# A Mamba-style decoder layer in which VectorE reads du from SBUF, Silu is one activation, and GpSimd's products have a new place

## The chip, the cores and the metric

The kernel runs on 1 core of one Trainium2 chip. The metric is the device time of one execution in microseconds (us). The kernel before was timed three times: 1171.12, 1177.21 and 1181.13 us, median 1177.21.

## The reference, cut to what matters

One decoder layer with four sequences (batches) of 512 tokens and 512 features: a selective state space block, then an attention over the context, then a linear layer with weights and rows quantized to integers; behind each an addition and a layer norm. The change touches the first block alone.

```python
proj = einsum('blh,he->bel', x, W_in)
hidden, gate = split(proj, 2, axis=1)              # E = 1024 channels each
hidden = silu(causal_conv4(hidden) + conv_bias)
dt, B, C = split(einsum('ble,ed->bld', hidden.T, W_x), [128, 144])
dts = softplus(dt @ W_dt + b_dt)                   # (b, l, E)
dA  = exp(dts[..., None] * A)                      # A: E x 16 states
dBu = dts[..., None] * B[:, :, None, :] * hidden[..., None]
state = dA * state + dBu                           # along the 512 tokens
y = einsum('ben,bn->be', state, C)
out = ((y + hidden * D) * silu(gate)) @ W_out
```

## The kernel before

The state scan has 4 x 1024 x 16 rows of 512 tokens. It is cut into 128 units, 32 a batch (UNITS). A unit is 32 channels of one batch with their 16 states: 128 partitions are 32 channels x 4 states, and the 4 (NJ) columns of 512 tokens hold the other states. Four units make the 128 channels of a block e (8 blocks a batch).

For one unit u:
- SyncE copies the 32 rows of dts and of du = dts * hidden from `steps` four times into `rep[u % REPS]` (`repeat`, line 348), by DMA.
- ScalarE computes dA in four exponentials (`exps`, line 581), one unit ahead of VectorE (AHEAD = 4 exponentials), and copies du from `rep` to the PSUM bank `du_rep` (`spread`, line 592). There is one such bank: the copy for u+1 waits until VectorE has finished the products of u.
- VectorE (`unit`, line 787) multiplies du, broadcast over two columns, by B from the SBUF tensor `Bb` into the PSUM tensor `dBu`, twice (line 798), and then runs two scans of 1024 elements (line 804) into `st[u % RING]`, with RING = 6.
- GpSimd multiplies each half of `st` by C from `Cb` in place (line 464).
- After four units TensorE sums the states in `state_sum` (line 927) with small matmuls into a bank `dense`.

All engines walk the same list of steps (b, g): step g of batch b goes with unit 32b + g + 1. What else a step does is in `items` (line 66), from tables of positions: projections "h" and "g" of the next and the current batch, the convolution "c" (four matmuls on TensorE from `pj`), "z" (softplus of the steps of a block on ScalarE, then du on GpSimd, line 492), the state sum "y", and for the batch before the output product "wo", attention ("q", "k", "en", "at", "xt", "av") and the quantized product ("qt", "ff"). Each such product takes one of BANKS = 3 PSUM banks in turn. In each step an engine does the unit's work first, then pending work of the last step, then the items.

Silu is built from tanh, since x * sigmoid(x) = x/2 * (1 + tanh(x/2)). For a gate ScalarE does tanh, the halving and the plus one (lines 698, 699, 701) and GpSimd the product (503). For a convolution ScalarE does the same three (565, 566, 568) and GpSimd the product one step later (478). For the first batch the convolution runs on VectorE (line 773) with taps and bias halved ahead of it (831, 832), then tanh and plus one (548, 550) and GpSimd's product. The exponentials, the softplus and the tanh need activation tables: a load stands in the program where the needed set is not the active one.

The first unit of batches 1 to 3 (STAGED = 1) takes B and C from the two halves of `wide`, since `Bb` and `Cb` can be loaded only once the last unit of the batch before is through (`load_bc`, line 340). As soon as VectorE and GpSimd have read `wide` for this unit (semaphores `s_mul` and `s_p`, line 394), SyncE loads w_out (2 MB) into it (`load_w_out`, line 337). TensorE needs it for "wo" at g = 2, and VectorE adds that product to the rows in `add_rows` (line 763). All the DMAs of this stretch stand in SyncE's one queue.

## Time and profile before

| what | value |
|---|---|
| median of 3 timed executions | 1177.21 us (1171.12 to 1181.13) |
| the profiled execution | 1177.67 us |
| its span, first to last instruction | 1175.9 us |
| mean granted TensorE clock | 0.859 of full speed |
| instructions in the profile | 10334 |
| packets of DMA, bytes | 66684, 135.03 MB |

The profile is of one execution. Busy shares are of the span. PE is TensorE, DVE is VectorE, ACT is ScalarE, POOL is GpSimd, SP is SyncE. A line number is that of the kernel before. In a group, the last columns are the idle time of the engine just ahead of these instructions and what ended most of it. A timeline row merges neighbours of one group: "4.45 ... x2" is the time from the start of the first to the end of the second.

### The profile page before, as it was taken

Reading aid. Unit: us, or ns where it says so; the run is one execution under the profiler, and the core shown is the slowest. Engines: PE = TensorE matmul, PEld = TensorE weight load, DVE = VectorE, ACT = ScalarE, POOL = GpSimd, SP = SyncE. Lnnn points to the kernel's source line nnn. Section 1 sums busy time; section 2 is a strip of 40 time slices with the busy share of each in tenths; the row PEclk is TensorE's granted clock in tenths of the full one; section 3 lists DMA queues with packets and bytes.
Section 4 is the critical chain, followed back from the end, with each engine's and each line's share of the span. In section 5 each row is a group of like instructions: output and inputs, shape, how many; then the busy total and the mean of one; then the engine's idle time right before and its main releaser. Section 6 shows DMA issues by size and latency. Waiting matters only on the chain.

```text
span 1175.9 us, 10334 instructions
## 1 busy us (share of the span) xinstructions
PE 856.8 (73%) x2708; PEld 335.0 (28%) x2718; DVE 973.5 (83%) x783; ACT 792.3 (67%) x1336; POOL 774.6 (66%) x483
## 2 busy tenths in 40 slices
PE   7923488878369789976639789878629856666994
PEld 2311133322023233432214234333203323222331
DVE  2469999898789987888979987898878999999733
ACT  3456677776456886886647777785666677777446
POOL 2228777777567766778656775777666777686533
PEclk9976698889679999998769898998868978777997
DMA  5184444453972334253893343344594353225100
GB/s 177 36 198 104 103 113 110 107 137 86 242 205 67 102 92 108 72 146 83 214 261 77 85 110 80 88 121 108 132 274 102 75 153 91 63 63 143 28 0 37
DMA packets 66684, 135.03 MB, mean 115 GB/s; under 512 B 13120, under 2 KB 19392, under 8 KB 66624
## 3 DMA queue, kind: packets, MB, share of 16 engines
q1 hardware_dynamic: 65904, 134.28, 45.0%
q8 instruction: 22, 0.36, 0.1%
q14 instruction: 38, 0.31, 0.1%
q10 hardware_dynamic: 720, 0.08, 0.0%
HBM read 62.75 MB, written 4.46 MB: 57 GB/s over the span
## 4 chain that ended last, share of the span: by engine, by line
PE 26%; issue 25%; DVE 20%; ACT 15%; DMA 7%; POOL 5%; SPq 1%; DVEq 0%; ACTq 0%; POOLq 0%
PE dense L906 16%; DVE st L804 14%; PE dense L962 6%; ACT dA L589 5%; POOL st L464 4%; DMA rep<-steps 3%; DMA wide<-w_out 3%; DVE dBu L798 2%; PE dense L939 2%; ACT squares L620 1%; DVE hs L782 1%; DVE x L763 1%; ACT L577 1%; ACT du_rep L597 1%; PE dBu L916 1%
## 5 line engine op out<-in xcount | busy, mean ns | idle before, releaser
L464 POOL TENSOR_TENSOR st<-st,Cb 128x1024 f32<-128x1024 f32 x250 | 584.3, 2359 | 216.5 <-DVE st L804 173.7
L804 DVE TENSOR_TENSOR_SCAN st<-dA,dBu 128x1024 f32<-128x1024 f32 x256 | 570.0, 2268 | 0.3 <-ACT dA L589 0.3
L589 ACT ACTIVATE dA<-rep,Aneg 128x511 f32<-128x511 f32 x512 | 328.0, 710 | 84.7 <-DMA rep<-steps 56.4
L798 DVE TENSOR_TENSOR dBu<-du_rep,Bb 128x1024 f32<-128x1024 f32 x250 | 294.4, 1223 | 78.9 <-ACT du_rep L597 46.4
L906 PE MATMUL dense<-xTs,Win 128*128 128x512 f32 x512 | 239.4, 612 | 14.2 <-DMA xTs<-xT 7.8
L939 PE MATMUL dense<-st,sel 128*32 128x512 f32 x1024 | 131.1, 657 | 52.1 <-POOL st L464 52.1
L906 PE MATMUL dense<-wide,hs 128*128 128x512 f32 x256 | 122.0, 633 | 61.9 <-DMA wide<-w_out 39.2
L906 PEld LDWEIGHTS dense<-xTs,Win 128*128 128x128 f32 x512 | 97.6, 195 | 147.3 <-issue 146.6
L962 PE MATMUL dense<-pj,Win 128*128 128x512 f32 (+1 forms) x192 | 105.5, 701 | 34.2 <-DVEq L785 20.7
L597 ACT COPY du_rep<-rep 128x512 f32<-128x512 f32 x128 | 74.3, 581 | 57.0 <-DVE dBu L798 48.6
L503 POOL TENSOR_TENSOR ta<-ta,tb 128x512 f32<-128x512 f32 x32 | 41.1, 1284 | 77.4 <-ACT tb L701 77.4
L906 PEld LDWEIGHTS dense<-wide,hs 128*128 128x128 f32 x256 | 51.0, 204 | 131.0 <-issue 68.1
L939 PEld LDWEIGHTS dense<-st,sel 128*32 128x32 f32 x1024 | 32.2, 119 | 149.6 <-issue 85.0
L962 PEld LDWEIGHTS dense<-pj,Win 128*128 128x128 f32 x192 | 42.2, 228 | 95.1 <-issue 95.0
L478 POOL TENSOR_TENSOR hs<-tb,ta 128x512 f32<-128x512 f32 x32 | 40.7, 1272 | 38.9 <-ACT tb L550 38.9
L933 PE MATMUL dense<-hs,Ddiag 128*128 128x512 f32 x64 | 38.0, 679 | 30.2 <-DVEq L785 22.4
L630 ACT ACTIVATE x<-x,nmean,rstd 128x512 f32<-128x512 f32 x36 | 28.8, 814 | 43.9 <-POOL nmean L472 43.9
L698 ACT ACTIVATE tb<-dense 128x512 f32<-128x512 f32 x32 | 19.0, 593 | 52.7 <-PE dense L906 48.0
L924 PE MATMUL dense<-ident,small 128*128 128x128 f32 x128 | 23.8, 318 | 41.4 <-ACT small L638 29.5
L492 POOL TENSOR_TENSOR steps<-steps,hs 128x512 f32<-128x512 f32 x32 | 40.7, 1271 | 19.6 <-ACT steps L577 19.6
L906 PE MATMUL dense<-wide 128*128 128x512 f32 x96 | 46.2, 626 | 6.2 <-ACTq L579 5.4
L906 PE MATMUL dense<-hs,wide 128*128 128x512 f32 x80 | 42.5, 687 | 11.1 <-issue 10.3
(112 smaller groups left out, 845.4 us busy)
## 6 DMA issues: line engine op xcount, KB each, us to landing
rep<-steps SPq DMA_DIRECT2D x512, 128.0 KB, 2.7
Win<-w_in SPq DMA_DIRECT2D x64, 256.0 KB, 2.7
wide<-w_out SPq DMA_DIRECT2D x4, 2048.0 KB, 16.4
Win<-w_conv SPq DMA_DIRECT2D x24, 256.0 KB, 2.6
wide<-bc_rows SPq DMA_DIRECT2D x24, 256.0 KB, 6.3
xTs<-xT SPq DMA_DIRECT2D x4, 1024.0 KB, 10.8
Bb<-bc_rows SPq DMA_DIRECT2D x16, 256.0 KB, 11.1
Cb<-bc_rows SPq DMA_DIRECT2D x16, 256.0 KB, 12.2
```

Of the source, the lines that this page charges most:

```text
L464: nc.gpsimd.tensor_tensor(s, s, C[:, j, :], ALU.mult).then_inc(s_p, 1)
L478: nc.gpsimd.tensor_tensor(hs[:, kb % 2, i, :], tb[:, m, :], ta[:, m, :], ALU.mult).then_inc(s_hs, 1)
L492: nc.gpsimd.tensor_tensor(steps[:, n % 3, 1, :], steps[:, n % 3, 0, :], hs[:, kb % 2, i, :], ALU.mult).then_inc(s_du, 1)
L503: nc.gpsimd.tensor_tensor(a, a, t, ALU.mult).then_inc(s_gate, 1)
L589: nc.scalar.activation(dA[:, u % 2, j, 1:T], rep[:, u % REPS, 0, 1:T], ACT.Exp, scale=Aneg[:, u % UNITS, j:j + 1]).then_inc(s_dA, 1)
L597: nc.scalar.copy(du_rep[:], rep[:, u % REPS, 1, :]).then_inc(s_duf, 1)
L798: V.tensor_tensor(dBu[:, j, :], du_rep[:].unsqueeze(1).to_broadcast([P, JH, T]), B[:, j, :], ALU.mult).then_inc(s_mul, 1)
L804: V.tensor_tensor_scan(st[:, u % RING, j, :].rearrange("p j t -> p (j t)"), dA[:, u % 2, j, :].rearrange("p j t -> p (j t)"), dBu[:, j, :] ...
L906: mm = nc.tensor.matmul(ps[0:rows, :], lhsT, rhs, start=n == 0, stop=n == len(pairs) - 1)
L933: nc.tensor.matmul(ps, Ddiag[:, e, :], hs[:, b % 2, e, :], start=True, stop=False)
L939: mm = nc.tensor.matmul(ps[32 * q:32 * q + 32, :], sel[:, 0:32], st[:, (4 * n + q) % RING, j, :], start=False, stop=j == NJ - 1)
L962: mm = nc.tensor.matmul(ps[:, k:T], Win[:, n % 3, k, :], pj[:, 0:T - k], start=k == 0, stop=k == KC - 1)
```

## The change

- VectorE's products read du from `rep` in SBUF; `spread`, `du_rep` and its semaphore are gone. `rep` has 4 buffers instead of 3, and the buffer is free when VectorE's products are done.
- The PSUM bank of `du_rep` becomes a fourth bank `dense`.
- Silu is one activation for the convolutions (in both forms) and for the gate; the halvings, the plus ones, the tensor `tb` and GpSimd's products `hs` and `ta` are gone.
- GpSimd's product for the first half of a unit keeps its place. The one for the second half stands at the end of the step, behind norms, du and the bias, and waits until VectorE has finished both products of the next unit.

```diff
-BANKS = 3
-REPS = 3
+BANKS = 4
+REPS = 4
...
-                    sp.wait_ge(s_duf, u - REPS + 1)
+                    sp.wait_ge(s_mul, NH * (u - REPS + 1))
...
+            def weigh_states(u, h):
+
+                C = spread_at(pool, u, s_cc, 1, Cb)
+                pool.wait_ge(s_scan, NH * u + h + 1)
+                if h and u + 1 < NB * UNITS:
+                    pool.wait_ge(s_mul, NH * (u + 2))
+                j = slice(JH * h, JH * h + JH)
+                s = st[:, u % RING, j, :]
+                nc.gpsimd.tensor_tensor(s, s, C[:, j, :], ALU.mult).then_inc(s_p, 1)
...
-                    C = spread_at(pool, u, s_cc, 1, Cb)
-                    for h in range(NH):
-                        pool.wait_ge(s_scan, NH * u + h + 1)
-                        j = slice(JH * h, JH * h + JH)
-                        s = st[:, u % RING, j, :]
-                        nc.gpsimd.tensor_tensor(s, s, C[:, j, :], ALU.mult).then_inc(s_p, 1)
+                scanned = 0 <= u < NB * UNITS
+                if scanned:
+                    weigh_states(u, 0)
...
-                for kb, i in pending:
-
-                    pool.wait_ge(s_tanh, 2 * (NE * kb + i + 1))
-                    m = temp[("c" if kb else "h", kb, i)] % TEMPS
-                    nc.gpsimd.tensor_tensor(hs[:, kb % 2, i, :], tb[:, m, :], ta[:, m, :],
-                                            ALU.mult).then_inc(s_hs, 1)
...
-                        pool.wait_ge(s_gt, 3 * (n + 1))
-                        nc.gpsimd.tensor_tensor(a, a, t, ALU.mult).then_inc(s_gate, 1)
-                        pool.wait_ge(s_gate, n + 1)
                     if key in norm:
                         rows.append(key)
+                if scanned:
+                    weigh_states(u, 1)
...
-                nc.scalar.activation(t, ps, ACT.Tanh, scale=0.5, bias=cb[:, i:i + 1]).then_inc(s_tanh, 1)
-                nc.scalar.activation(a, ps, ACT.Identity, scale=0.5, bias=cb[:, i:i + 1]).then_inc(free, 1)
-                act.wait_ge(s_tanh, n + 1)
-                nc.scalar.activation(t, t, ACT.Identity, bias=ones[:, 0:1]).then_inc(s_tanh, 1)
+                nc.scalar.activation(hs[:, b % 2, i, :], ps, ACT.Silu, bias=cb[:, i:i + 1]).then_inc(s_hs, 1)
+                act.wait_ge(s_hs, NE * b + i + 1)
+                act.sem_inc(free, 1)
...
-            def spread(u):
-
-                act.wait_ge(s_rep[u % REPS], 64 * (u // REPS + 1))
-                if u:
-                    act.wait_ge(s_mul, NH * u)
-                nc.scalar.copy(du_rep[:], rep[:, u % REPS, 1, :]).then_inc(s_duf, 1)
...
-                        nc.scalar.activation(t, ps, ACT.Tanh, scale=0.5).then_inc(s_gt, 1)
-                        nc.scalar.activation(a, ps, ACT.Identity, scale=0.5).then_inc(s_gt, 1)
-                        act.wait_ge(s_gt, 3 * n + 2)
-                        nc.scalar.activation(t, t, ACT.Identity, bias=ones[:, 0:1]).then_inc(s_gt, 1)
+                        nc.scalar.activation(temp_slot(key), ps, ACT.Silu).then_inc(s_gate, 1)
+                        act.wait_ge(s_gate, NE * kb + i + 1)
                         act.sem_inc(free, 1)
...
             def unit(u):
-                dve.wait_ge(s_duf, u + 1)
+                dve.wait_ge(s_rep[u % REPS], 64 * (u // REPS + 1))
...
-                    V.tensor_tensor(dBu[:, j, :], du_rep[:].unsqueeze(1).to_broadcast([P, JH, T]), B[:, j, :],
+                    V.tensor_tensor(dBu[:, j, :], rep[:, u % REPS, 1:2, :].to_broadcast([P, JH, T]), B[:, j, :],
                                     ALU.mult).then_inc(s_mul, 1)
```

The order on GpSimd at steps 10 to 12 of batch 0, the kernel before: du of a block (L492), the products with C (L464), and the products that finish a convolution (L478) and a gate (L503).

```order
L492 TENSOR_TENSOR steps<-steps,hs 128x512 [waits steps_ready]
L464 TENSOR_TENSOR st<-st,Cb 128x1024 [waits scan_done] x2
L478 TENSOR_TENSOR hs<-tb,ta 128x512 [waits tanh_done]
L503 TENSOR_TENSOR ta<-ta,tb 128x512 [waits hs_ready,gate_part]
L464 TENSOR_TENSOR st<-st,Cb 128x1024 [waits scan_done,gate_ready]
L464 TENSOR_TENSOR st<-st,Cb 128x1024 [waits scan_done]
L478 TENSOR_TENSOR hs<-tb,ta 128x512 [waits tanh_done]
```

The same place of the changed kernel, where L480 is du and L456 the products with C.

```order
L456 TENSOR_TENSOR st<-st,Cb 128x1024 [waits scan_done]
L480 TENSOR_TENSOR steps<-steps,hs 128x512 [waits hs_ready,steps_ready]
L456 TENSOR_TENSOR st<-st,Cb 128x1024 [waits dBu_done,scan_done]
L456 TENSOR_TENSOR st<-st,Cb 128x1024 [waits scan_done]
L456 TENSOR_TENSOR st<-st,Cb 128x1024 [waits dBu_done,scan_done]
```

du has moved between the two products of its unit, the second product of every unit waits for VectorE's products as well (dBu_done), and the products of the convolution and the gate are gone.

The order on ScalarE at steps 10 and 11 of batch 0, the kernel before: softplus (L577), convolution (L565 to L568), `pj` (L558), exponentials (L589), the copy of du (L597).

```order
L577 ACT_TABLE_LOAD
L577 ACTIVATE steps<-dense0,bdt 128x512
L565 ACT_TABLE_LOAD
L565 ACTIVATE tb<-dense1,cb 128x512
L566 ACTIVATE ta<-dense1,cb 128x512
L568 ACTIVATE tb<-tb,ones 128x512
L558 COPY pj<-dense2 128x512
L589 ACTIVATE dA<-rep,Aneg 128x511 x4
L597 COPY du_rep<-rep 128x512
```

The same place of the changed kernel (softplus L556, convolution L545, `pj` L540, exponentials L568, gate L663).

```order
L556 ACT_TABLE_LOAD
L556 ACTIVATE steps<-dense0,bdt 128x512
L545 ACT_TABLE_LOAD
L545 ACTIVATE hs<-dense1,cb 128x512
L540 COPY pj<-dense2 128x512
L568 ACT_TABLE_LOAD
L568 ACTIVATE dA<-rep,Aneg 128x511 x4
L545 ACT_TABLE_LOAD
L545 ACTIVATE hs<-dense3,cb 128x512
L663 ACTIVATE ta<-dense0 128x512
```

Two activations and the copy have gone, and a table load has come behind the convolution and ahead of the next one. Over the whole program the order has 63 loads before and 139 in the changed kernel.

The order on GpSimd at the first batch boundary of the changed kernel, where the first unit of the batch takes C from `wide`.

```order
L456 TENSOR_TENSOR st<-st,wide 128x1024 [waits scan_done,bc_staged]
L456 TENSOR_TENSOR st<-st,wide 128x1024 [waits dBu_done,scan_done,bc_staged]
L456 TENSOR_TENSOR st<-st,Cb 128x1024 [waits scan_done,c_spread]
```

The second product with `wide`, for which the load of w_out waits, now stands behind VectorE's products of the next unit, which need `Bb`.

## Rows read from the trace of the kernel before

**Rows 1.** The page, part 1; then one stretch: us, busy us by engine, PEclk, DMA, GB/s
```profile
PE 856.8 (73%) x2708; PEld 335.0 (28%) x2718; DVE 973.5 (83%) x783; ACT 792.3 (67%) x1336; POOL 774.6 (66%) x483
...
72.42:1119.20 1046.78, 761.46 (x2439) 297.20 (x2449) 930.20 (x698) 730.79 (x1216) 740.26 (x424) 0.85 0.48 120
```

**Rows 2.** Groups of instructions by line: busy us, mean ns, idle before
```profile
L804 DVE TENSOR_TENSOR_SCAN st<-dA,dBu 128x1024 f32<-128x1024 f32 x256 | 570.0, 2268 | 0.3 <-ACT dA L589 0.3
L798 DVE TENSOR_TENSOR dBu<-du_rep,Bb 128x1024 f32<-128x1024 f32 x250 | 294.4, 1223 | 78.9 <-ACT du_rep L597 46.4 <-DMA Bb<-bc_rows 17.1 <-DVE x L763 6.0
...
L464 POOL TENSOR_TENSOR st<-st,Cb 128x1024 f32<-128x1024 f32 x250 | 584.3, 2359 | 216.5 <-DVE st L804 173.7 <-DMA Cb<-bc_rows 40.9 <-POOL hs L478 0.4
...
L597 ACT COPY du_rep<-rep 128x512 f32<-128x512 f32 x128 | 74.3, 581 | 57.0 <-DVE dBu L798 48.6 <-DMA rep<-steps 8.4
```

**Rows 3.** Timeline 290 to 300 us, VectorE and GpSimd: start, us, what
```profile
290.32 2.34 DVE L798 TENSOR_TENSOR dBu<-du_rep,Bb 128x1024 f32<-128x1024 f32 x2
292.56 4.46 DVE L804 TENSOR_TENSOR_SCAN st<-dA,dBu 128x1024 f32<-128x1024 f32 x2
...
294.92 4.65 POOL L464 TENSOR_TENSOR st<-st,Cb 128x1024 f32<-128x1024 f32 x2 [1.86 <-DVE st L804]
```

**Rows 4.** Waits of VectorE, 72.42 to 1119.2 us: total, times, longest
```profile
DVE dBu L798 <- ACT du_rep L597: 49.4, 28, 10.8
DVE x L763 <- PE dense L906: 22.3, 5, 6.7
DVE dBu L798 <- DMA Bb<-bc_rows: 17.1, 3, 6.4
DVE dense L890 <- PE dense L906: 7.3, 4, 3.5
DVE x L763 <- issue: 6.6, 2, 3.3
```

**Rows 5.** Timeline 54 to 61 us, VectorE and GpSimd
```profile
54.67 1.01 DVE L756 TENSOR_SCALAR small<-x,winv 128x512 f32<-128x512 f32 x2
...
58.61 0.70 DVE L756 TENSOR_SCALAR small<-x,winv 128x512 f32<-128x512 f32 x1 [2.93 <-PE dense L924]
...
59.34 1.46 DVE L756 TENSOR_SCALAR small<-x,winv 128x512 f32<-128x512 f32 x1
...
57.75 1.27 POOL L492 TENSOR_TENSOR steps<-steps,hs 128x512 f32<-128x512 f32 x1 [4.01 <-ACT steps L577]
59.25 1.26 POOL L492 TENSOR_TENSOR steps<-steps,hs 128x512 f32<-128x512 f32 x1 [0.23 <-ACT steps L577]
```

**Rows 6.** GpSimd: groups by line, and a timeline row
```profile
L492 POOL TENSOR_TENSOR steps<-steps,hs 128x512 f32<-128x512 f32 x32 | 40.7, 1271 | 19.6 <-ACT steps L577 19.6
...
L470 POOL TENSOR_TENSOR rstd<-var,neghalf 128x1 f32<-128x1 f32 x48 | 26.5, 552 | 35.3 <-ACT var L623 35.3
...
L472 POOL TENSOR_TENSOR nmean<-nmean,rstd 128x1 f32<-128x1 f32 x48 | 9.2, 192 | 3.8
...
52.47 1.26 POOL L478 TENSOR_TENSOR hs<-tb,ta 128x512 f32<-128x512 f32 x1 [4.20 <-ACT tb L550]
```

**Rows 7.** Timeline at the first batch boundary, all engines
```profile
309.51 4.68 POOL L464 TENSOR_TENSOR st<-st,wide 128x1024 f32<-128x1024 f32 x2 [1.13 <-DVE st L804]
...
314.26 0.40 SPq L338 DMA_DIRECT2D wide<-w_out  x1
...
317.98 2.36 DVE L798 TENSOR_TENSOR dBu<-du_rep,Bb 128x1024 f32<-128x1024 f32 x2 [6.44 <-DMA Bb<-bc_rows]
...
341.85 0.69 DVE L763 SCALAR_TENSOR_TENSOR x<-dense,x 128x512 f32<-128x512 f32 x1 [2.98 <-PE dense L906]
```

**Rows 8.** ScalarE: timeline at a table load; the gate's plus one
```profile
471.74 1.28 ACT L577 ACT_TABLE_LOAD   x1
473.03 0.69 ACT L577 ACTIVATE steps<-dense,bdt 128x512 f32<-128x512 f32 x1
...
L701 ACT ACTIVATE tb<-tb,ones 128x512 f32<-128x512 f32 x32 | 23.1, 722 | 1.0
```

More of the change, by code:

```diff
@@ L50 @@
 HID_AT = [9, 10, 13, 14, 17, 18, 21, 22]
+CONV_AT = [10, 11, 14, 15, 18, 19, 22, 23]
 DT_AT = 25
@@ L84, in items @@
         keys.append(("z", (n + 2) // NE, (n + 2) % NE))
-    if after and b >= 0 and g - 1 in HID_AT:
-        keys.append(("c", b + 1, HID_AT.index(g - 1)))
-    if after and g in HID_AT:
-        keys.append(("h", b + 1, HID_AT.index(g)))
+    if after and b >= 0:
+        keys.extend(("c", b + 1, i) for i, at in enumerate(CONV_AT) if at == g)
+    if after:
+        keys.extend(("h", b + 1, i) for i, at in enumerate(HID_AT) if at == g)
     if b >= 1:
@@ L122, in decoder_layer @@
     turn = {key: (n % BANKS, n // BANKS) for n, key in enumerate(order)}
-    temp_keys = [key for key in order if key[0] in "gc" or key[0] == "h" and key[1] == 0]
+    temp_keys = [key for key in order if key[0] == "g" or key[0] == "h" and key[1] == 0]
     temp = {key: m for m, key in enumerate(temp_keys)}
@@ L485, in _ @@
                     n = NE * kb + i
-                    a, t = (x[:, temp[key] % TEMPS, :] for x in (ta, tb)) if key in temp else (None, None)
-                    if kind == ("c" if kb else "h"):
-                        pending = [(kb, i)]
-                    elif kind == "z":
+                    if kind == "z":
                         pool.wait_ge(s_dt, n + 1)
+                        pool.wait_ge(s_hs, n + 1)
                         nc.gpsimd.tensor_tensor(steps[:, n % 3, 1, :], steps[:, n % 3, 0, :], hs[:, kb % 2, i, :],
@@ L531, in temp_slot @@
                     else:
-                        act.wait_ge(s_temp, sum(k[0] != "g" for k in temp_keys[:m - TEMPS + 1]))
-                return ta[:, m % TEMPS, :], tb[:, m % TEMPS, :]
+                        act.wait_ge(s_hs, i + 1)
+                return ta[:, m % TEMPS, :]
             def hid_front(b, i):
                 ps, _ = full(("h", b, i))
-                a, _ = temp_slot(("h", b, i))
-                if b == 0 and i == 0:
-                    act.wait_ge(s_prep, 1)
+                a = temp_slot(("h", b, i))
+                if i == 0:
+                    act.wait_ge(s_conv_c, 32)
                 nc.scalar.activation(a, ps, ACT.Identity, scale=ck[:, i, KC - 1:KC],
@@ L546, in hid_back @@
                 act.wait_ge(s_conv, NE * b + i + 1)
-                t = tb[:, m, :]
-                nc.scalar.activation(t, ta[:, m, :], ACT.Tanh).then_inc(s_tanh, 1)
-                act.wait_ge(s_tanh, 2 * (NE * b + i) + 1)
-                nc.scalar.activation(t, t, ACT.Identity, bias=ones[:, 0:1]).then_inc(s_tanh, 1)
+                nc.scalar.activation(hs[:, b % 2, i, :], ta[:, m, :], ACT.Silu).then_inc(s_hs, 1)
             def projected(b, i):
@@ L657, in _ @@
                     first = NJ * (UNITS * b + g + 1)
-                    u = first // NJ
-                    if u == 0:
-                        spread(0)
                     for m in range(first + AHEAD if first else 0, min(first + NJ + AHEAD, NB * UNITS * NJ)):
                         exps(m // NJ, m % NJ)
-                    if u + 1 < NB * UNITS:
-                        spread(u + 1)
                 for args in pending:
```

21 lines of the change are left out of this document (1 added, 20 removed).

## The prediction

> **What bounds the kernel now.** I read the page's busy times first. VectorE is busy for 83% of the span, every other engine for 73% or less [rows 1]. The stretch that matters runs from the first product of a unit to the last scan, 72.4 to 1119.2 us: 1046.8 us, with VectorE busy for 930.2 of them [rows 1]. A unit is two products (state inputs dBu) and two scans [rows 2]. In the timeline the next product starts as the last scan ends: 290.32 to the scan at 292.56, and 4.46 us of scans [rows 3]; a unit costs about 6.64 us (2.26 to the scan, 4.38 to the next product), and 128 units 850 us. The other VectorE work in the stretch is 930.2 - 850 = 80 us. The remaining 117 us are waits. Their list [rows 4] shows the copy of du into PSUM first: 49.4 us in 28 places, of which the longest, 10.8, lies ahead of the stretch; so 38.6 inside. Then 22.3 + 7.3 + 6.6 = 36.2 us for products of TensorE, and 17.1 for Bb at the batch boundaries. So VectorE is the bound, and the copy the largest wait.
>
> **VectorE's source of du.** The copy goes: 128 on ScalarE (74.3 us, [rows 2]), which is no bound, and with it the waits of 38.6 us. They go whole: without the first they are 27 of 1.4 us on average, and come about because a copy is the last thing in ScalarE's step, behind the exponentials of the same unit. Now VectorE's product needs no engine but the DMA of `rep`, and only its scan, 2.3 us behind, needs the exponentials. The product itself keeps 1024 elements a lane. No product of that shape from two SBUF tensors is in the trace; between the 512-element operation of 486 ns [rows 5] doubled (0.97) and GpSimd's 2.36 us for the same shape [rows 2], I take its own 1.22 [rows 2], nearest by far.
>
> **The two engines' products.** What the change adds is that this product reads rep and Bb, both in SBUF, while GpSimd multiplies two SBUF tensors. One place shows what VectorE can suffer from that [rows 5]. A SBUF-to-SBUF operation of 512 elements takes 0.49 us at 54.67, GpSimd idle (two in 1.01). At 58.61 it takes 0.70 and ends 0.29 after GpSimd's product ends (57.75 + 1.27 = 59.02). The next starts at 59.34, takes 1.46 and ends at 60.80: again 0.29 after GpSimd's (59.25 + 1.26 = 60.51). So this kind waits for the end of a GpSimd operation, and 0.49 - 0.29 = 0.20 us of its own lead lie inside the wait. It has one tensor input, so it does not prove the case; from below the cost of such waits is nothing, and from above the full serial sum (below). I take it that they exclude each other, as the only rows on the question do.
> The Trainium skill, SBUF — State Buffer, "Who interferes with whom", speaks against the change: a VectorE instruction with two SBUF inputs contends with a GpSimd one that reads SBUF, and whichever comes second blocks until the first is over. By that rule the sum below stands; without it the first rival does. The trace agrees for the one-input kind (+0.29 us both times).
>
> The new order places GpSimd's second product of unit u behind both VectorE products of u+1, and small GpSimd work ahead of it. I follow a plain unit from the start S of its first scan. The last product ends at S + 0.10 (2.34 for the two against 2.24 to the scan, [rows 3]); GpSimd follows 0.1 later (it starts at 294.92 where the first scan ended at 292.56 + 2.27 = 294.83, [rows 2, 3]). Its pair takes 4.68 [rows 7], so GpSimd is done at S + 4.88, where VectorE was done at S + 4.45: it blocks 0.4 us. First product 1.22 - 0.20 later, S + 5.90; second 1.12 later, S + 7.02; next scan S + 6.93. Instead of 6.64, 6.93 us: 128 units take 887.
> Extras come on top. VectorE's (80 us) hide the 0.45 us that GpSimd lasts longer, wherever one stands: 53 us stay over, counted unit by unit along the order. GpSimd's lie between its two products of a unit, where VectorE wants the same exclusion: 30 products du of 1.27 (38 us), 12 additions of the bias of the same shape (15), 36 pairs of 0.55 and 0.19 for the norms (27) [rows 6]. They mostly fall on units where VectorE has no extra. All serial, where the larger of the two counts in a unit: 53 + 78 = 131; if the second and later one of a place slips beside the next scan, about half of the 42 us that are not du goes: 111. I take 111.
>
> **Waits that stay or come.** Bb 17. TensorE's 36: a fourth bank lets it run ahead, I take 10 off (between none and the 26 not at w_out), 26. At each of three boundaries the load of w_out waits for GpSimd's second product of the staged unit. Before, that ran from 309.51, and the load was issued at 314.26, ahead of VectorE's next product at 317.98, which waited for Bb. Now the product stands behind it: 317.98 + 2.36 + 2.36, so w_out is issued at 322.7, 8.4 us later. VectorE waited 2.98 us for the product with w_out at 341.85 [rows 7]; with fewer transfers beside it I take w_out 6 us later, half of it hidden by VectorE's own delay: 3 x 3 = 9. The load of Cb waits likewise, one product (2.4 us) later, which shifts GpSimd against a VectorE product: 3 x 2 = 6. At the start GpSimd begins late, behind the load of Cb (it waits 40.9 us in all for Cb, [rows 2]), and must catch up two units, each product against one of VectorE's: 4. Sum 62.
> Stretch: 887 + 111 + 62 = 1060 against 1046.8: +13.
>
> **ScalarE and Silu.** Each gate, and each convolution from the second batch on, falls from three activations to one (gate: tanh, half, plus one). The order has 139 table loads instead of 63. A load takes 1.28 us and the next activation starts 0.01 later [rows 8]: 76 x 1.283 = 98 us more. Against that stand the 74 of the copies [rows 2], and two activations less for each of the 32 gates and 24 convolutions: the plus one, 0.72 [rows 8], and the halving, at least the 0.58 of a copy of that shape [rows 2], 56 x 1.30 = 73. ScalarE gets no busier (98 against 147), and it is idle for 30% of the stretch (730.8 of 1046.8 busy, [rows 1]). Cost 0; the cover is that idle time and the lead of one unit that the exponentials have. If it is gone, a load (1.28) stands ahead of the exponentials and the scan waits for them.
> The Trainium skill, ScalarE: Activation LUTs, "What ACT_TABLE_LOAD costs", states some 1.38 us of drain beside each load; by it ScalarE would carry 105 us more. The row at 473.03 stands directly behind the load [rows 8], so this trace shows no drain there.
> In the head the last hs needs no plus-one (0.72) and no product on GpSimd (1.27) [rows 6, 8]: -2 us.
>
> **Sum.** Profiled execution 1177.7 (span 1175.9) + 13 - 2 = 1189, say 1190; the median of the three is 1177.2, half a microsecond lower, so nothing is moved for it.
>
> **Rivals.**
> - *No exclusion for two SBUF inputs.* For it: those rows show only the one-input kind. Then the copy's waits go and nothing replaces them: 1177.7 - 38.6 - 10 - 2, plus w_out late in full, 3 x 6 = 18: 1145. Chance 0.13.
> - *The exclusion is dearer.* GpSimd wins at every change of hands: all 131 us serial (+20), 0.1 us at each of 256 VectorE products (+26), TensorE's 10 not won: 1246; with half of it 1220. Against it: a waiting VectorE got in at once at 59.02 [rows 5]. Chance 0.25.
> - *The extras hide.* All of GpSimd's but du slip beside scans (-21): 1169. Chance 0.14.
> - *ScalarE becomes late* by its loads: a third of 98 us on the path, 1222. VectorE's waits before [rows 4] name no exponential. Chance 0.03.
> The forecast holds 0.45.
>
> **Numbers.** A measurement tells about 1% from no change, 12 us. Faster (below 1165): the first rival and a part of the third, 0.20. Same: 0.28, from the third and the lower part of the forecast's (1165 to 1189). Slower: 0.52. The range goes from the first rival, 1145, to 1228, between the two sizes of the second.
>
> **What would show it.** The products of VectorE (1.22 us) have a longer mean, about 1.5, with the first of each unit near 1.4 to 1.7 and ending 1.0 us after a GpSimd product; no wait for du is left; 139 loads of 1.28; w_out issued one VectorE and one GpSimd product behind Bb. If the products stay at 1.22 beside GpSimd, the first rival holds and the forecast is wrong. If waits for dA at scans appear, it is ScalarE.

## The result and the profile after

The changed kernel took 1164.9 us (median of four executions, 1162.72 to 1165.72) against 1178.8 us before in the same comparison (four, 1171.12 to 1181.13): a ratio of 0.990, interval 0.986 to 0.994. It is faster by 1%, where 1190 us and a loss of 1% were forecast. Its profiled execution took 1165.72 us.

The first part of its page, and below it the row for the stretch from the first product of a unit to the last scan, as in [rows 1]:

```profile
PE 830.5 (71%) x2708; PEld 327.9 (28%) x2718; DVE 1026.1 (88%) x781; ACT 759.5 (65%) x1164; POOL 748.2 (64%) x419
...
71.27:1107.80 1036.53, 736.50 (x2443) 290.64 (x2453) 983.23 (x698) 702.82 (x1053) 724.74 (x369) 0.87 0.48 121
```

The stretch fell from 1046.8 to 1036.5 us. VectorE's busy time in it rose by 53.0 us (930.2 to 983.2) with the same 698 instructions, and its idle time fell by 63.3 (116.6 to 53.3). That is nearly the whole result: 53 us of something that the records count as work, against 63 us of waits. ScalarE's busy time in the stretch fell, from 730.8 to 702.8.

The groups by line show where the 53 us lie. They answer to [rows 2, 6].

```profile
L767 DVE TENSOR_TENSOR_SCAN st<-dA,dBu 128x1024 f32<-128x1024 f32 x256 | 570.0, 2266 | 0.0
...
L761 DVE TENSOR_TENSOR dBu<-rep,Bb 128x1024 f32<-128x1024 f32 x250 | 344.9, 1423 | 37.9 <-DMA rep<-steps 10.9
...
L480 POOL TENSOR_TENSOR steps<-steps,hs 128x512 f32<-128x512 f32 x32 | 57.6, 1799 | 72.8 <-ACT steps L556 72.7
...
L469 POOL TENSOR_TENSOR rstd<-var,neghalf 128x1 f32<-128x1 f32 x48 | 49.4, 1028 | 42.5 <-ACT var L595 42.5
```

The scans are unchanged to 2 ns. The 250 products of VectorE went from a mean of 1223 to 1423 ns, which is 50 us. On the other side GpSimd's du went from 1271 to 1799 and its small rstd from 552 to 1028. A mean that rises for the same shape on two engines at once suggests that each stands still inside its own instruction. The timeline shows it: first VectorE, then GpSimd, 94 to 106 us.

```profile
94.94 2.72 DVE L761 TENSOR_TENSOR dBu<-rep,Bb 128x1024 f32<-128x1024 f32 x2
...
101.95 3.80 DVE L761 TENSOR_TENSOR dBu<-rep,Bb 128x1024 f32<-128x1024 f32 x2
...
90.80 4.64 POOL L456 TENSOR_TENSOR st<-st,Cb 128x1024 f32<-128x1024 f32 x2 [1.23 <-DVE dBu L761]
97.81 4.64 POOL L456 TENSOR_TENSOR st<-st,Cb 128x1024 f32<-128x1024 f32 x2 [2.37 <-DVE dBu L761]
102.41 2.25 POOL L480 TENSOR_TENSOR steps<-steps,hs 128x512 f32<-128x512 f32 x1
```

GpSimd's pair ends at 95.44, half a microsecond into VectorE's pair at 94.94; that pair takes 2.72 instead of 2.34 [rows 3]. The next GpSimd pair ends at 102.45, and du is queued right behind it. VectorE's pair at 101.95 gets its first product in, du waits meanwhile (2.25 instead of 1.27) and runs between the two products, and VectorE's pair takes 3.80. In these rows each engine waits for the end of the other's current instruction, then goes first. From here on this is called the block. Counted over the timeline, 58 of the 128 pairs took 2.3 to 2.4 us, 44 took 2.7 to 2.8 (0.4 more), four 3.0 to 3.2, 21 took 3.4 to 4.0, and one 6.10. All pairs together took 356 us, against 301 both in the kernel before and in the kernel that has the new place but whose products still read PSUM (place_alone, below).

All 21 long pairs come from a du. In 16 of them du lies inside the pair. In the other five du ran first and made GpSimd's two products with C late, so that the end of the second one falls into VectorE's pair. One of the five:

```profile
416.33 3.65 DVE L761 TENSOR_TENSOR dBu<-rep,Bb 128x1024 f32<-128x1024 f32 x2
...
411.87 1.27 POOL L480 TENSOR_TENSOR steps<-steps,hs 128x512 f32<-128x512 f32 x1 [2.63 <-ACT steps L556]
413.10 4.66 POOL L456 TENSOR_TENSOR st<-st,Cb 128x1024 f32<-128x1024 f32 x2
```

VectorE's waits in that stretch, which answer to [rows 4]:

```profile
DVE x L726 <- PE dense L866: 13.7, 5, 4.0
DVE dBu L761 <- DMA rep<-steps: 10.9, 1, 10.9
...
DVE x L726 <- issue: 6.3, 2, 3.5
DVE dBu L761 <- DMA Bb<-bc_rows: 6.1, 3, 3.7
DVE dBu L761 <- PE dense L899: 5.2, 3, 3.8
```

The wait for the copy is gone. The 10.9 for `rep` is one wait ahead of the first product and no part of the 53.3. Bb fell from 17.1 to 6.1. TensorE's two at `x` (13.7 + 6.3 = 20.0) stood at 28.9, and the 7.3 at L890 fell to 0.4 (now L850). The 5.2 for the state sums (L899) is the 5.3 that the kernel before has at L939 and that [rows 4] does not show.

A small part of the wait for du has come back in another form.

```profile
DVE dBu L761 <- issue: 5.1, 3, 2.2
```

The view names no cause for these three. The two longest end at 427.24 and 693.17 us, and the last DMA that fills `rep` for that unit lands at 426.89 and 692.76. So VectorE waits there for `rep` itself.

### The profile page after: what moved, and what is told of

It reads as the page before. It is cut to its first block, busy times and chain, and to the rows that moved or that the text cites. A ratio compares the mean times of both kernels' runs of the same rounds, so it can differ in the third digit from the quotient of the medians.

```text
span 1163.9 us, 10065 instructions
## 1 busy us (share of the span) xinstructions
PE 830.5 (71%) x2708; PEld 327.9 (28%) x2718; DVE 1026.1 (88%) x781; ACT 759.5 (65%) x1164; POOL 748.2 (64%) x419
## 4 chain that ended last, share of the span: by engine, by line
issue 35%; DVE 28%; PE 22%; DMA 6%; ACT 5%; POOL 2%; SPq 2%; DVEq 0%; POOLq 0%; ACTq 0%
DVE st L767 19%; PE dense L866 15%; DVE dBu L761 4%; PE dense L922 3%; DMA wide<-w_out 2%; DMA Bb<-bc_rows 2%; PE dense L899 2%; DVE x L726 1%; DVE hs L745 1%; POOL st L456 1%; PE dBu L876 1%; SPq L340 1%; DVE xsc L818 1%; DVE dense L850 1%; ACT squares L592 1%
## 5 line engine op out<-in xcount | busy, mean ns | idle before, releaser
L456 POOL TENSOR_TENSOR st<-st,Cb 128x1024 f32<-128x1024 f32 x250 | 584.5, 2360 | 279.3 <-DVE dBu L761 256.0
L568 ACT ACTIVATE dA<-rep,Aneg 128x511 f32<-128x511 f32 x512 | 329.3, 710 | 119.9 <-DVE st L767 110.7
L761 DVE TENSOR_TENSOR dBu<-rep,Bb 128x1024 f32<-128x1024 f32 x250 | 344.9, 1423 | 37.9 <-DMA rep<-steps 10.9
L899 PE MATMUL dense<-st,sel 128*32 128x512 f32 x1024 | 134.2, 665 | 112.8 <-POOL st L456 112.8
L922 PE MATMUL dense<-pj,Win 128*128 128x512 f32 (+1 forms) x192 | 94.5, 638 | 32.4 <-issue 22.2
L480 POOL TENSOR_TENSOR steps<-steps,hs 128x512 f32<-128x512 f32 x32 | 57.6, 1799 | 72.8 <-ACT steps L556 72.7
L899 PEld LDWEIGHTS dense<-st,sel 128*32 128x32 f32 x1024 | 31.0, 117 | 209.3 <-POOL st L456 134.7
L469 POOL TENSOR_TENSOR rstd<-var,neghalf 128x1 f32<-128x1 f32 x48 | 49.4, 1028 | 42.5 <-ACT var L595 42.5
L922 PEld LDWEIGHTS dense<-pj,Win 128*128 128x128 f32 x192 | 37.9, 205 | 86.8 <-issue 86.8
L884 PEld LDWEIGHTS dense<-ident,small 128*128 128x128 f32 x128 | 17.0, 162 | 105.4 <-ACT small L610 66.2
L726 DVE SCALAR_TENSOR_TENSOR x<-dense,x 128x512 f32<-128x512 f32 x36 | 24.7, 686 | 21.0 <-PE dense L866 13.7
L663 ACT ACTIVATE ta<-dense 128x512 f32<-128x512 f32 x32 | 19.1, 597 | 33.2 <-PE dense L866 32.7
```

The costliest lines, as they stand in the source:

```text
L456: nc.gpsimd.tensor_tensor(s, s, C[:, j, :], ALU.mult).then_inc(s_p, 1)
L469: nc.gpsimd.tensor_tensor(rstd[:, c], var[:, c], neghalf[:], ALU.pow).then_inc(s_rstd, 1)
L480: nc.gpsimd.tensor_tensor(steps[:, n % 3, 1, :], steps[:, n % 3, 0, :], hs[:, kb % 2, i, :], ALU.mult).then_inc(s_du, 1)
L568: nc.scalar.activation(dA[:, u % 2, j, 1:T], rep[:, u % REPS, 0, 1:T], ACT.Exp, scale=Aneg[:, u % UNITS, j:j + 1]).then_inc(s_dA, 1)
L726: V.scalar_tensor_tensor(x_i, ps, 1.0, x_i, ALU.mult, ALU.add, accum_out=rowsum[:, n % 4:n % 4 + 1]).then_inc(s_sum, 1)
L761: V.tensor_tensor(dBu[:, j, :], rep[:, u % REPS, 1:2, :].to_broadcast([P, JH, T]), B[:, j, :], ALU.mult).then_inc(s_mul, 1)
```

## The experiments

The times are medians, the ratio is to the kernel before on the same chip, with its 95% interval. Two runs, marked so, are single executions. Sums of pairs, idle times and stretches are read from the one profiled execution of each kernel.

### Is the block real, and is it the source in SBUF?

**place_undone**: the changed kernel, but GpSimd's second product right behind the first, without its new wait.

```diff
             def weigh_states(u, h):
-                if h and u + 1 < NB * UNITS:
-                    pool.wait_ge(s_mul, NH * (u + 2))
...
                     weigh_states(u, 0)
+                    weigh_states(u, 1)
...
-                if scanned:
-                    weigh_states(u, 1)
```

> The changed kernel with GpSimd's second product of each unit put back directly behind the first, without the wait for VectorE's products. Theory A (exclusion, and the waiting VectorE gets in between two GpSimd products): VectorE's two products are split by one GpSimd product of 2.34 us, pairs near 4.9 instead of 2.75, some 2.2 us more for each of 128 units: 1165 + 200 to 280, about 1400. Rival B (VectorE keeps its turn for both products, or the place is of little worth): under 1200.

1306.3 us (one execution), 141 us above the changed kernel: 1.10 us a unit. VectorE, then GpSimd, from its timeline:

```profile
108.96 4.70 DVE L758 TENSOR_TENSOR dBu<-rep,Bb 128x1024 f32<-128x1024 f32 x2
...
106.94 5.63 POOL L454 TENSOR_TENSOR st<-st,Cb 128x1024 f32<-128x1024 f32 x2 [1.14 <-DVE st L764]
```

The pair takes twice its 2.34 us, and GpSimd's pair 5.63 instead of 4.65. GpSimd starts at 106.94 and ends its first product at about 109.3; VectorE, ready at 108.96, gets in then; GpSimd's second product, queued since 109.3, gets in between VectorE's two. Nothing in either instruction has changed against the changed kernel, only when they meet. Theory A had the mechanism right and the size too large: 61 of the 128 pairs took 4.6 to 5.0 us, where it expected all of them near 4.9. The pairs sum to 519 us, 162 more than in the changed kernel, and VectorE's waits fell by 18.

**place_alone**: the kernel before, du still copied to PSUM, with only the new place and wait of GpSimd's second product.

```diff
+                scanned = 0 <= u < NB * UNITS
+                if scanned:
+                    weigh_states(u, 0)
...
+                if scanned:
+                    weigh_states(u, 1)
```

> The kernel before (du copied to PSUM, tanh, three banks) with only the place of GpSimd's second product changed: behind the small work of the step and behind VectorE's products of the next unit. Theory A (exclusion needs two SBUF inputs; here VectorE's product has one): VectorE's products stay at 1.22 us, pairs at 2.34, though GpSimd's work of 1.27 us now lies beside them; the time moves only through later state sums and w_out, 1174 to 1190. Rival B (GpSimd's work stretches VectorE's products whatever their source): pairs of 2.7 us and more, and a time over 1200.

1176.3 us against 1177.95, 0.998 (0.997 to 1.000): the place alone is worth nothing. Its groups and its waits:

```profile
L805 DVE TENSOR_TENSOR dBu<-du_rep,Bb 128x1024 f32<-128x1024 f32 x250 | 294.3, 1223 | 74.0 <-ACT du_rep L604 40.7 <-DMA Bb<-bc_rows 17.2 <-DVE x L770 6.7
```
```profile
DVE dBu L805 <- ACT du_rep L604: 43.0, 22, 10.3
```

All 128 pairs took 2.3 or 2.4 us, the sum 301.4, as theory A expected, though GpSimd's products stand where they stand in the changed kernel. The cleanest comparison is with tanh_kept (below), which differs from this kernel only in the source of du (and with it the copy on ScalarE) and in the fourth bank: there the pairs sum to 415 us and the time is 1232.5. With du from PSUM there is no block; with both inputs from SBUF there is.

**narrow_products**: the changed kernel with GpSimd's products with C cut to one element a column. It leaves out nearly all of the products with C.

```diff
-                nc.gpsimd.tensor_tensor(s, s, C[:, j, :], ALU.mult).then_inc(s_p, 1)
+                nc.gpsimd.tensor_tensor(s[:, :, 0:1], s[:, :, 0:1], C[:, j, 0:1], ALU.mult).then_inc(s_p, 1)
```

> The changed kernel, but GpSimd's products with C take one column of each 512 instead of all (it leaves out nearly all of the products with C). Theory A (exclusion: VectorE's products are long, 356 us in all instead of 301, only because of GpSimd's operations): pairs of 2.37 nearly everywhere but beside du, the sum of VectorE's products falls to 310 to 320, the time to about 1125. Rival B (the product from two SBUF tensors is itself slower, or something else stretches it): pairs keep their 2.75 us. If the products shorten and the time stays over 1150, TensorE is the next bound.

1135.4 us (one execution), 29.5 below the changed kernel.

```profile
L456 POOL TENSOR_TENSOR st<-st,Cb 128x2 f32<-128x2 f32 x250 | 49.2, 198 | 777.3 <-DVE dBu L761 530.8 <-DVE st L767 209.5 <-DMA Cb<-bc_rows 29.0
...
L761 DVE TENSOR_TENSOR dBu<-rep,Bb 128x1024 f32<-128x1024 f32 x250 | 313.3, 1298 | 45.9 <-PE dense L899 12.9 <-DMA Bb<-bc_rows 12.5 <-DMA rep<-steps 9.9
```

The pairs now sum to 320 us, 36 less, and 114 of 128 are free of any block. In the stretch the time fell by 27 of these 36: nine came back as waits, mostly for TensorE (12.9 instead of 5.2) and Bb (12.5 instead of 6.1). So GpSimd's products with C cost the changed kernel about 27 us through the block; the rest of the 29.5 lies ahead of the stretch and behind it. The 19 us that remain above 301 lie in the 14 pairs of 3.2 to 4.2 us, all with a du, six of them with the bias as well. Theory A's sum (310 to 320) is met and rival B falls, since the same two products from SBUF take 2.3 to 2.4 us when GpSimd is out of the way; the time is 10 us above the 1125 expected.

### What Silu is worth

**silu_alone**: the kernel before, with Silu as one activation, in the changed kernel's steps for the convolutions, and nothing else (copy of du, three banks, three buffers).

```diff
-                nc.scalar.activation(t, ps, ACT.Tanh, scale=0.5, bias=cb[:, i:i + 1]).then_inc(s_tanh, 1)
...
+                nc.scalar.activation(hs[:, b % 2, i, :], ps, ACT.Silu, bias=cb[:, i:i + 1]).then_inc(s_hs, 1)
```

> The kernel before with Silu as one activation and the table of positions for the convolution, nothing else (the copy of du into PSUM, three banks and three rep buffers stay, GpSimd's second product stays directly behind the first). Theory A (the gain of the change lies in the copy of du and in VectorE's other waits; Silu is hidden apart from the head): 2 us less in the head and within 6 us of before otherwise, about 1176; VectorE's waits for the copy stay between 35 and 55 us. Rival B (the gain comes from ScalarE and GpSimd being freed of the tanh form): 1165 or less, the waits for the copy fall under 20 us.

1173.7 us against 1177.1, 0.995 (0.992 to 0.997). Theory A holds: a gain of 3.4 us where it expected about 2, and a wait for the copy that did not fall but grew, from 49.4 to 54.6. In the profiled executions the whole gain lies ahead of the stretch, which starts at 69.50 us instead of 72.42; the stretch itself is 1046.8 us long in both. Such a start is uncertain by itself: it lies at 71.27 in the changed kernel and at 68.79 in staged_now (below), whose program is the same up to there.

```profile
DVE dBu L772 <- ACT du_rep L575: 54.6, 34, 8.8
```

**tanh_kept**: the other half: du from `rep`, four banks (three buffers), the new place, but Silu still from tanh, with GpSimd's 64 products of 1.27 us for it.

```diff
-            def spread(u):
...
-                dve.wait_ge(s_duf, u + 1)
+                dve.wait_ge(s_rep[u % REPS], 64 * (u // REPS + 1))
...
+                if scanned:
+                    weigh_states(u, 1)
```

> The kernel before with the source of du, four banks and the new place of GpSimd's second product, but Silu as tanh as before and three rep buffers (a fourth does not fit beside tb). GpSimd keeps 56 products of 1.27 us for convolutions and gates. Theory A (each of them stands in VectorE's way like a product du, 0.8 to 1.1 us each, and Silu's worth in this change lies in that): 1205 to 1230. Rival B (Silu is worth what it is worth alone on the kernel before, 3 to 5 us): 1166 to 1172.

1232.5 us against 1175.7, 1.047 (1.044 to 1.050).

```profile
L791 DVE TENSOR_TENSOR dBu<-rep,Bb 128x1024 f32<-128x1024 f32 x250 | 403.8, 1659 | 40.0 <-DMA rep<-steps 9.9 <-DMA Bb<-bc_rows 8.3 <-DVE x L756 7.4
```
```profile
486.99 5.08 DVE L791 TENSOR_TENSOR dBu<-rep,Bb 128x1024 f32<-128x1024 f32 x2 [0.71 <-PE dense L932]
...
483.95 1.29 POOL L506 TENSOR_TENSOR ta<-ta,tb 128x512 f32<-128x512 f32 x1 [7.87 <-ACT tb L694]
485.31 5.66 POOL L459 TENSOR_TENSOR st<-st,Cb 128x1024 f32<-128x1024 f32 x2
```

The product with `ta` at 483.95 makes GpSimd's pair late; VectorE's pair at 486.99 falls on it and takes 5.08. The mean of VectorE's product is 1659 ns, 236 above the changed kernel's, 59 us over 250. Against the same kernel with Silu (reps3, below, 1163.2) it is 69 us slower, a little more than theory A's upper end. (GpSimd keeps 64 such products, 32 for convolutions and 32 for gates; the expectation counted 56.) So Silu is worth 3.4 us by itself and 69 beside the products from SBUF, and without it the change would have lost 5%. Nearly all of it acts through GpSimd, by taking 64 of its instructions away: against reps3 the pairs hold 60 us more and VectorE's waits 6, and no scan waits for dA.

### The wait for the copy

**copy_first**: the kernel before, with the copy of du ahead of the exponentials of its step instead of behind them.

```diff
+                        if m == max(first + AHEAD, NJ):
+                            spread(u + 1)
...
-                    if u + 1 < NB * UNITS:
-                        spread(u + 1)
```

> The kernel before with one thing moved: in ScalarE's step the copy of du for unit u+1 stands ahead of the four exponentials of u+1 instead of behind them. Theory A (most of the gain of the change is the wait for this copy, which came last in the step): the 38.6 us of waits inside the stretch fall to under 12, the time to about 1150, with VectorE's products at 1.22 us throughout. Rival B (these waits are those of a late ScalarE, so the scan's wait for the exponentials takes their place): within 1% of before, 1170 to 1182, with a new wait of scans for dA of 20 us or more.

1193.4 us, 1.011 (1.008 to 1.014). Both theories missed. First VectorE's waits, then ScalarE's group of the copy:

```profile
DVE dBu L798 <- PE dense L939: 33.2, 12, 3.8
...
DVE dBu L798 <- DMA Bb<-bc_rows: 22.9, 3, 8.2
...
DVE dBu L798 <- ACT du_rep L597: 12.4, 4, 8.8
```
```profile
L597 ACT COPY du_rep<-rep 128x512 f32<-128x512 f32 x128 | 75.1, 587 | 194.4 <-DVE dBu L798 160.2 <-DMA rep<-steps 33.5 <-ACT steps L577 0.7
```

The wait for the copy fell to 12.4 us, 8.8 of it ahead of the stretch, as theory A had it, but the time did not follow. The copy now holds ScalarE, 194 us in all (57.0 before, [rows 2]), mostly until VectorE has read the bank, and what stands behind it on ScalarE starts later. Rival B's new wait for dA is not there either (0.35 us at a scan). The waits of VectorE for TensorE's state sums appeared, 33.2 us. A cheaper cure of the wait in the old kernel than the changed source was thus not found here; where TensorE was held up was not traced further.

**silu_copy_first**: both together, 1175.9 us, 0.997 (0.995 to 1.000). The diff is that of the two above.

> Both of the two before: Silu as one activation, and the copy of du ahead of the exponentials. Theory A: the two add up, about 1148, faster than the changed kernel (1165), since nothing of VectorE's is blocked by GpSimd. Rival B: at best the changed kernel's time, 1165.

The copy's wait is 10.7 (one, ahead of the stretch), the state sums 27.5. With ScalarE relieved the same edit costs 2 us (against silu_alone) instead of 16, but still wins nothing; theory A, that the two add up to 1148, missed by 28 us.

### Banks, buffers, and the late w_out

**banks3** and **reps3**: the changed kernel with BANKS = 3, and with REPS = 3.

```diff
-BANKS = 4
+BANKS = 3
```

> The changed kernel with three dense banks instead of four (the fourth is left unused). Theory A (as predicted, the fourth bank is worth some 10 us): about 1175. Theory B (formed on the run with the copy ahead of the exponentials: with three banks TensorE comes late as soon as VectorE stops waiting for the copy, so the fourth bank carries most of the gain): 1185 or more, with VectorE waiting over 40 us more than in the changed kernel for TensorE (state sum L899 and the products).

> The changed kernel with three rep buffers instead of four. Theory A (a buffer is now held until VectorE's products are done, 2.3 us longer than for the copy; three are enough, since the DMA is issued two units ahead): within 3 us of the changed kernel, 1162 to 1168. Rival B: waits for rep at the batch boundaries, 5 us or more at each: 1180.

banks3 took 1172.7 us (0.996, 0.994 to 0.998), reps3 1163.2 (0.988, 0.985 to 0.991). The difference of the two is 9.6 us; against the changed kernel's own 1164.9, banks3 is 7.8 us slower. This is the worth of the fourth bank, since the fourth buffer of `rep` is worth nothing measurable. The first expectation of each run holds. In banks3:

```profile
DVE x L726 <- PE dense L866: 17.3, 5, 5.7
...
DVE dBu L761 <- PE dense L899: 15.4, 9, 3.8
```

against 13.7 and 5.2: the bank's worth is a wait for TensorE's state sums and one for its dense products.

**staged_now**: the changed kernel, where GpSimd's second product of a staged unit doesn't wait for VectorE's next products, so that w_out is loaded earlier.

```diff
-                if h and u + 1 < NB * UNITS:
+                if h and u + 1 < NB * UNITS and not (u and u % UNITS < STAGED):
```

> The changed kernel, but for the first unit of batches 1 to 3 (which reads the halves of wide) GpSimd's second product does not wait for VectorE's products of the next unit, so that the load of w_out is issued some 8 us earlier at three places. Theory A (the late w_out costs 3 us at each boundary, as in the prediction): 1156, and up to 18 us less (1147) if nothing hides it. Rival B (the load lands faster, w_out is not late for VectorE by more than before): within 3 us of the changed kernel, 1162 to 1168.

1164.5 us, 0.987 (0.984 to 0.991): the same as the changed kernel, as rival B expected. w_out is issued at 320.02 and there at 335.6, 15.6 us later. In the changed kernel, at the same boundary (to be set beside [rows 7]):

```profile
322.28 2.37 DVE L761 TENSOR_TENSOR dBu<-rep,Bb 128x1024 f32<-128x1024 f32 x2 [3.69 <-DMA Bb<-bc_rows]
324.82 2.34 POOL L456 TENSOR_TENSOR st<-st,wide 128x1024 f32<-128x1024 f32 x1 [5.78 <-DVE dBu L761]
...
327.23 0.40 SPq L333 DMA_DIRECT2D wide<-w_out  x1
...
336.93 9.27 PE L866 MATMUL dense<-wide,hs 128*128 128x512 f32 x16 [14.68 <-DMA wide<-w_out]
...
346.32 0.69 DVE L726 SCALAR_TENSOR_TENSOR x<-dense,x 128x512 f32<-128x512 f32 x1 [2.69 <-PE dense L866]
```

It is issued at 327.23 and there at 336.93, after 9.7 us. Issued 7.2 us later by the clock of the profile, it lands 1.3 us later; and VectorE's own product with Bb stands 1.4 us later as well (322.28 against 320.89), so relative to VectorE's work it is not late at all. By the time of its issue the loads of Bb and Cb have landed (322.20 and 327.06); in staged_now they were still under way (until 320.81 and 325.67). That they are what lengthened its load there is argued from this order. VectorE's wait of 2.69 us for the product with it is no longer than before (2.98).

### GpSimd's small operations

**small_more**: the changed kernel plus one [128x1] power a unit on GpSimd, between the two products with C; its result is not used.

```diff
                 if scanned:
                     weigh_states(u, 0)
+                    pool.wait_ge(s_xs, u)
+                    nc.gpsimd.tensor_tensor(spare[:], ones[:], neghalf[:], ALU.pow).then_inc(s_xs, 1)
```

> The changed kernel with one more operation of GpSimd in each unit, of one element a lane like those of the norms (0.55 us alone), between the first product and the place of the second. As the prediction priced them (the full 0.55 us in VectorE's way): 128 x 0.55 less what extras of VectorE cover, 1210 to 1235. Theory now (such an operation holds VectorE back only for the moment in which it reads, and slips between or beside VectorE's products): 1165 to 1178.

1168.8 us, 0.9925 (0.990 to 0.995): 4 us for 128 operations, 0.03 us each.

```profile
L467 POOL TENSOR_TENSOR spare<-ones,neghalf 128x1 f32<-128x1 f32 x128 | 142.0, 1109 | 0.0
```
```profile
131.07 2.73 DVE L765 TENSOR_TENSOR dBu<-rep,Bb 128x1024 f32<-128x1024 f32 x2
...
131.54 1.53 POOL L467 TENSOR_TENSOR spare<-ones,neghalf 128x1 f32<-128x1 f32 x1
133.04 1.88 POOL L484 TENSOR_TENSOR steps<-steps,hs 128x512 f32<-128x512 f32 x1
134.89 4.67 POOL L458 TENSOR_TENSOR st<-st,Cb 128x1024 f32<-128x1024 f32 x2
```

Unblocked it takes 0.55 us. Here its mean is 1.11 and the busy time 142 us, yet the pairs of VectorE sum to 353 us, no more than the changed kernel's 356. At 131.54 it waits about 1 us inside VectorE's products, whose pair takes the 2.73 of any plain unit. VectorE does not wait for it; it waits for VectorE. The measured time fits the new theory (1165 to 1178) and not the price that the prediction had used (1210 to 1235). The 4 us lie in waits of the stretch: 17.0 us for TensorE's products at `x` (13.7 in the changed kernel), 8.1 for its state sums (5.2) and 9.0 for Bb (6.1). Why those grew is not shown. What the rows do show is that the small operation and du push GpSimd's next pair to 134.89, 1.2 us behind the scan's start at 133.72, where a pair with nothing ahead of it starts 0.2 behind; so the states that TensorE sums are ready later.

**du_behind**: the changed kernel with GpSimd's second product ahead of du and the bias instead of behind them, so that du lies beside the scans.

```diff
+                if scanned:
+                    weigh_states(u, 1)
                 for key in items(b, g):
...
-                if scanned:
-                    weigh_states(u, 1)
```

> The changed kernel with GpSimd's du product, the bias additions and the waits for them behind the second product of the unit (the second product directly behind the norms' operations), so that they stand ahead of the next first product. Theory (the sum of GpSimd's work between VectorE's pairs decides, not its order): the same within 6 us, 1159 to 1171, with as many long pairs. Rival (a du product that cannot get between VectorE's two products costs less): under 1157.

1174.7 us, 0.998 (0.995 to 1.000): 10 us slower than the changed kernel, outside both expectations. The pairs sum to 353 us, 3 less than there, so the block got a little cheaper. The loss lies in waits:

```profile
DVE x L726 <- PE dense L866: 16.9, 5, 5.1
...
DVE dBu L761 <- DMA Bb<-bc_rows: 16.0, 3, 6.3
```

Bb is back at 16.0 us from 6.1. At the first boundary the loads of Bb are issued at 308.6 here and 308.7 there, and VectorE's product with it starts at 323.67 here, at 322.28 in the changed kernel; and the pair ahead of that wait takes 2.73 here and 3.81 there. A block of VectorE at that place is hidden by the load, and taking it away only lengthens the wait. The load itself is 1.4 us later because du is: the DMAs that fill `rep` wait for du, and all the loads stand behind them in SyncE's one queue. The first of the four loads just ahead of Bb in it is issued at 302.57 instead of 301.12. SyncE's waits for du, first in this kernel, then in the changed one:

```profile
SPq L351 <- POOL steps L482: 84.9, 27, 3.7
```
```profile
SPq L351 <- POOL steps L480: 9.1, 8, 1.9
```

One more place for du (z_one_earlier) has no time: with softplus and du one step earlier in each group of four (Z_AT = 1), the engines wait for each other in a circle. Whether VectorE's product for the gate would then have hidden a part of the block is open.

## Why the prediction was wrong in sign

**The mechanism was right.** The two engines exclude each other when VectorE reads both inputs from SBUF and GpSimd reads SBUF. narrow_products, place_undone and the step from place_alone to tanh_kept show it from three sides. The rule of the Trainium skill, SBUF — State Buffer, "Who interferes with whom", holds here for a product with two SBUF inputs (pairs of 2.72, 3.80 and 4.70 us for 2.34), and the first rival falls. The one-input rows of [rows 5], which the prediction took as agreement, were no test of that rule, which speaks of two inputs; these pairs are. The forecast size for the gain was nearly right too: 38.6 us of waits for the copy gone, though 5.1 came back as waits for `rep`; the fourth bank at 8 to 10 measured for 10 forecast; Silu's table loads without cost on ScalarE.

**The step that failed: "if the second and later one of a place slips beside the next scan, about half of the 42 us that are not du goes: 111. I take 111."** It prices GpSimd's norms and bias as 20 us in VectorE's way, and every du in full. The blocks were put at 37 (887 - 850) + 31 (111 - 80) = 68 us, of which du made 38, the norms and the bias 20, plain units what was left, 10. Measured from the pairs: 30 us in the 21 that a du lengthened; 18 in the 44 plain ones at 0.4; 1.6 in two pairs that a bias made late; 1.3 in two others; the start 3.7 (84.55, 6.10 us), forecast 4 and booked among the waits. Together 55, and 53 in VectorE's busy time. So du was 8 too dear and the plain units 8 too cheap, and the norms and the bias were wrong outright, 1.6 for 20. The norms were priced as if a [128x1] operation of 0.55 us kept VectorE out for 0.55; small_more measured 0.03. The 20 pairs that have norms inside took 2.72 to 2.81 us, as the other plain ones did (2.68 to 2.83). In all 44 the first product ends 1.09 us after GpSimd's, so 0.13 of its own time lies inside the wait, where the prediction took 0.20.

The rows that show it could be read only afterwards. In the changed kernel, VectorE and GpSimd at 478 us:

```profile
478.19 2.75 DVE L761 TENSOR_TENSOR dBu<-rep,Bb 128x1024 f32<-128x1024 f32 x2
...
478.66 1.54 POOL L469 TENSOR_TENSOR rstd<-var,neghalf 128x1 f32<-128x1 f32 x1
480.29 0.70 POOL L471 TENSOR_TENSOR nmean<-nmean,rstd 128x1 f32<-128x1 f32 x1
480.94 1.26 POOL L480 TENSOR_TENSOR steps<-steps,hs 128x512 f32<-128x512 f32 x1
482.17 1.25 POOL L487 TENSOR_TENSOR x<-x,small 128x512 f32<-128x512 f32 x1
```

the norms stretch to 1.54 and 0.70 inside VectorE's pair and thereby push du and the bias out beside the scan, where they cost nothing. The forecast had named this as its third rival, "the extras hide", at 1169 us and a chance of 0.14, but kept du at full price in every unit. That rival was the nearest to what happened.

**The waits.** This is the second step that failed. Forecast 62, measured 53.3 of idle time. Bb: 6.1, not 17. TensorE's waits that made up the 36: 20.4, not 26. w_out and Cb, 9 + 6: nothing (staged_now); the step took w_out 6 us later, and relative to VectorE's work it was not late at all. The start: booked here with 4, measured among the blocks. Against these 11 + 6 + 15 + 4 = 36 us of excess stands an omission: the list of waits in [rows 4] names 38.6 + 36.2 + 17.1 = 92 us of the 117 in the stretch. The other 25 (5.3 for the state sums, 2.4 more for TensorE, and for the rest mostly waits of some 0.2 us and less) were dropped from the sum of the kernel after, where 27 us of this kind stand, the 5.1 for `rep` among them. Had the 25 been kept, the forecast would have been 1215 and not 1190. The error was hidden by terms that were too dear. In all, the stretch was forecast 23.5 us too long: 15 in the blocks, 9 in the waits. Without them the forecast would have had the right sign.

**Blocks that lie ahead of a wait.** They were summed as if each microsecond of block were a microsecond of path. At the boundaries the block lies ahead of a wait for Bb and is hidden (du_behind), and narrow_products gave back 36 us of block for 27 in the stretch. There a quarter of the block was covered. That a part of Bb's 11 us is this same cover is likely, but not measured.

**ScalarE.** 139 table loads of 1.283 us instead of 63, and no wait for it came up. The load at 477.82, with the activations ahead of it and behind it:

```profile
477.03 0.69 ACT L556 ACTIVATE steps<-dense,bdt 128x512 f32<-128x512 f32 x1
477.82 1.28 ACT L545 ACT_TABLE_LOAD   x1
479.11 0.69 ACT L545 ACTIVATE hs<-dense,cb 128x512 f32<-128x512 f32 x1
```

The activation starts 0.01 us behind the load, and the load starts 0.10 us behind the activation ahead of it (477.72). The drain of 1.38 us that the Trainium skill gives in ScalarE: Activation LUTs, "What ACT_TABLE_LOAD costs", is not seen, as in [rows 8].

**What the change is made of, then.** The new source of du takes away the waits for the copy and brings the block. Undone alone, the place costs 141 us, Silu 69, the fourth bank 8 to 10; done alone on the kernel before, the place brings 1.7 us, not clear of nothing, and Silu 3.4. With the source changed and either Silu or the place missing, the kernel loses (1232.5 and 1306.3 us). The source by itself and the fourth bank by itself were not run on the kernel before. The gain of 12 to 14 us is what 53 us of block leave of 63 us of waits.

## What to carry to other kernels

Before moving an operand of VectorE from PSUM to SBUF, list what GpSimd does at that moment: in these runs long instructions on both sides each waited for the other's end and stretched to nearly the sum, and [128x1] ones of GpSimd cost almost nothing. A long one costs even where it runs beside the scans, if it makes the next long one late. The placing and thinning out of GpSimd's long instructions was then worth many times what it was worth by itself, so such parts have to be priced together and not one by one. And when a list of waits is turned into a sum, close it against the idle time of the stretch: what the list doesn't name stays.

## What the runs showed that was not expected

- A block is booked as busy time. VectorE's busy share rose from 83 to 88% with the same 698 instructions in the stretch, and GpSimd's rstd doubled its mean, 552 to 1028 ns; none of it appears among the waits.
- The two engines take turns. In the rows shown, when both have an instruction ready, the one that was kept out goes next, even between two back-to-back products of the other: du between VectorE's products at 101.95 (3.80 us), GpSimd's product between them at 108.96 in place_undone (4.70).
- The [128x1] operations of GpSimd don't keep VectorE out in any way the pairs show (0.03 us each over 128), though they are kept out themselves for up to 1 us.
- A load of 2 MB issued 7 us later landed 1.3 us later: it took 9.7 us instead of 15.6, with fewer loads under way beside it.
- Moving du by one place on GpSimd slowed the loads: SyncE's waits for it rose from 9.1 to 84.9 us (du_behind), and through its one queue this reached the load of Bb.
